# GpSimd's gathers also wait for TensorE's signal of the quad two back

## The reference

```python
x = _layernorm(x + _L0_gnn_ref(...))   # attention: scores from K[src], Q[dst] and edge features; sums of V[src]*score by dst
x = _layernorm(x + _L1_gnn_ref(...))   # mean of x[src] and maximum of relu(x @ W_pool + b)[src] by dst, two matmuls, batch norm
x = _layernorm(x + _L2_gnn_ref(...))   # sum of ci * x[src] by dst, a matmul
x = _layernorm(x + _L3_gnn_ref(...))   # sum of edge_weight * (x @ W)[src] by dst, bias, norm
```

## Time and profile before

| | before |
|---|---|
| median of three runs | 4448.03 us |
| profiled execution | 4444.6 us |
| its span | 4442.8 us |
| GpSimd busy | 3209.6 us (72%) |
| TensorE busy | 2622.2 us (59%) |
| VectorE busy | 1994.1 us (45%) |
| ScalarE busy | 1397.3 us (31%) |
| first gather of pass 1, 2, 3, 4 | 42.1, 1191.9, 2321.7, 3379.0 us |

### The profile page before, as it was taken

How to read it: one execution, slowest core, us unless ns; L and a number is a source line. 1 busy time by engine, 2 the same in 40 slices (tenths; PEclk the granted TensorE clock), 3 DMA queues, 4 the chain that set the end, 5 groups by cost and what they waited for, 6 DMA issues and landing times.

```text
span 4442.8 us, 56823 instructions
## 1 busy us (share of the span) xinstructions
PE 2622.2 (59%) x15402; PEld 2238.4 (50%) x15402; DVE 1994.1 (45%) x4498; ACT 1397.3 (31%) x4325; POOL 3209.6 (72%) x3366
## 2 busy tenths in 40 slices
PE   6777887887676667666756643343344333344435
PEld 5666666666566666666634433333343333333334
DVE  3766666666576666666661111111124222222225
ACT  1222222224444444444453322222222222222223
POOL 4777777776277777777757777777776777777776
PEclk7999889897588888888875555555555555555556
DMA  6876676766333333333312122211122111121112
GB/s 192 221 189 184 182 185 182 185 185 170 96 102 99 99 99 99 101 100 99 97 40 40 40 40 40 40 40 40 40 44 51 40 40 39 40 40 39 40 40 55
DMA packets 337337, 409.95 MB, mean 92 GB/s; under 512 B 212209, under 2 KB 248676, under 8 KB 336942
## 3 DMA queue, kind: packets, MB, share of 16 engines
q0 software_dynamic: 133120, 245.58, 23.3%
q1 hardware_dynamic: 203917, 160.75, 13.5%
HBM read 386.26 MB, written 19.77 MB: 91 GB/s over the span
## 4 chain that ended last, share of the span: by engine, by line
POOL 32%; issue 27%; PE 23%; DVE 11%; DMA 5%; ACT 1%; SPq 1%; ACTq 0%; DVEq 0%; POOLq 0%
POOL rows L547 31%; PE bank L639 18%; DVE same L1534 5%; DVE same L1234 3%; DMA rows<-kv_table,src_idx 2%; PE bank L840 1%; DMA rows<-pair_table,src_idx 1%; DVE prod L1306 1%; DVE score L1308 1%; POOL acc_max L574 1%; DVE prod L1304 1%; PE bank L684 1%; PE bank L652 0%; PE bank L653 0%; PE bank L744 0%
## 5 line engine op out<-in xcount | busy, mean ns | idle before, releaser
L639 PE MATMUL bank<-same,rows 128*96 128x128 f32 x4992 | 1086.0, 389 | 1123.9 <-issue 1044.0
L639 PEld LDWEIGHTS bank<-same,rows 128*96 128x96 f32 x4992 | 926.3, 248 | 1257.4 <-issue 1251.5
L547 POOL DMA_INDIRECT rows<-kv_table,src_idx x832 | 793.7, 954 | 318.8 <-issue 238.9
L547 POOL DMA_INDIRECT rows<-pair_table,src_idx x832 | 787.0, 946 | 317.5 <-issue 249.2
L927 ACT COPY acc<-bank 96x511 f32 (+1 forms) x832 | 481.0, 578 | 1647.1 <-PE bank L639 1645.8
L547 POOL DMA_INDIRECT rows<-h_table,src_idx x832 | 790.2, 950 | 272.3 <-issue 253.3
L547 POOL DMA_INDIRECT rows<-ci_table,src_idx x832 | 785.0, 944 | 261.6 <-issue 253.3
L1234 DVE TENSOR_TENSOR same<-bank,rank_col 128x512 f32<-128x512 f32 x624 | 422.9, 678 | 842.7 <-PE bank L639 842.7
L1534 DVE TENSOR_SCALAR same<-iota_s,rank_col,src_hi 128x128 f32<-128x128 f32 x832 | 240.4, 351 | 754.5 <-PE bank L639 754.3
L639 PEld LDWEIGHTS bank<-same,msg 128*105 128x105 f32 x1664 | 232.1, 197 | 306.6 <-DVE same L1234 199.2
L652 PE MATMUL bank<-weights,first_only 97*128 97x96 f32 x1664 | 355.5, 299 | 38.6 <-DMA first_only<-q_table 32.8
(11 more groups left out here) (169 smaller groups left out, 3241.4 us busy)
## 6 DMA issues: line engine op xcount, KB each, us to landing
first_only<-in_attr_cols SPq DMA_DIRECT2D x104, 384.0 KB
first_only<-q_table SPq DMA_DIRECT2D x832, 48.0 KB
first_only<-rank_rows SPq DMA_DIRECT2D x104, 256.0 KB
first_only<-keep_rows SPq DMA_DIRECT2D x104, 192.0 KB, 3.1
rows<-kv_table,src_idx POOLq DMA_INDIRECT x832
rows<-pair_table,src_idx POOLq DMA_INDIRECT x832
rows<-ci_table,src_idx POOLq DMA_INDIRECT x832
rows<-h_table,src_idx POOLq DMA_INDIRECT x832
```

Source lines behind the costliest of these rows:

```text
L547: pool.indirect_dma_start(rows[:, k, j, 0:width], None, table, bass.IndirectOffsetOnAxis(ap=src_idx[:, t:t + 1], axis=0)).then_inc(rows_in ...
L639: mm = pe.matmul(out[0:nrow, here], left(j), right(j), start=(j == 0), stop=(j == TQ - 1), skip_group_check=True)
```

## The change

`edge_pass_pool` gets two more arguments, a semaphore `paced` and a number `behind`. Before the first gather of quad q it waits, besides the free buffer, until `paced` has been raised for quad q - 2. With `behind = 2` quads 0 and 1 of a pass have no such wait. `paced` is `q_done` in pass 1, `turn_done` in pass 2 and `agg_done` in passes 3 and 4, where it is also the semaphore of the buffer wait.

```diff
-        def edge_pass_pool(pool, table, width, freed):
+        def edge_pass_pool(pool, table, width, freed, paced, behind):
             for q in range(NQ):
                 k = q % GQ
                 wait(pool, freed, q - GQ + 1)
+
+                wait(pool, paced, q - behind + 1)
                 for j in range(TQ):
...
-            edge_pass_pool(pool, kv_table, KV, msg_done)
+            edge_pass_pool(pool, kv_table, KV, msg_done, q_done, 2)
...
-            edge_pass_pool(pool, pair_table, PAIR, passes[1].agg_done)
+            edge_pass_pool(pool, pair_table, PAIR, passes[1].agg_done, turn_done, 2)
...
-            edge_pass_pool(pool, ci_table, F, passes[2].agg_done)
+            edge_pass_pool(pool, ci_table, F, passes[2].agg_done, passes[2].agg_done, 2)
...
-            edge_pass_pool(pool, h_table, F, passes[3].agg_done)
+            edge_pass_pool(pool, h_table, F, passes[3].agg_done, passes[3].agg_done, 2)
```

## The result

| | before | after |
|---|---|---|
| median of four runs each | 4446.34 us | 4475.46 us |
| lowest to highest | 4444.19 to 4450.7 us | 4472.38 to 4478.1 us |
| profiled execution | 4444.6 us | 4478.0 us |
| its span | 4442.8 us | 4476.2 us |

The ratio on record is 1.0061, 95% interval 1.0049 to 1.0072: 29 us slower by the medians, where 12.8 were forecast.

A forecast was written before the change was run, and what follows sets the result against it. GpSimd's gather issue rate was taken as the bound. Delays at the starts of pass 1 (5.6) and pass 2 (7.2), all else 0, sum to +12.8 us: 4461 us predicted, range 4448 to 4473 (forecast alone 4456 to 4467).

The forecast's parts named there:

- Who bounds the kernel: All passes: GpSimd's issue rate, 5.0 us a quad; its lateness in mid-pass reaches the pass end one for one.
- the tail: End of pass 1, quads 201 to 207: held by the new wait, but 7.4 us against 18, cost 0.
- Pass 1, start, +5.6: Pass 1, quads 10 and 11: quad 11 starts 5.57 us late, all reaching consumers; bounds 3.3 to 6.5.
- rival A: Pass 1 and 2 starts: held gathers free the DMA engines, giving part of the delay back; 4452 to 4456, chance 0.18.
- Pass 2, start, +7.2: Pass 2, quad 2: waits for the late first turn, starting at 1209.08 instead of 1201.85; all 7.2 us reach the tail.
- Rival B: Pass 1 mainly: gathers get shorter, so not slower, about 4444 us; chance 0.06.
- Passes 3 and 4, middle, 0: Signal of two quads back comes 1.72 us before the gather, 0.73 is needed: wait already met, cost 0.
- The added wait as an instruction: From each pass's fifth quad, about 816 extra sequencer instructions: taken as 0, bounds 0 to 326 us.
- The comparison of 0.73 with 1.72: Middle of passes 3 and 4: signal-to-gather time 0.73 us is below the signal's 1.72 us lead, so cost 0.
- Rival C: All passes: each of 816 added wait instructions shows at 30 ns, 25 us on top of 12.8, about 4486; chance 0.08.
- Rival D: Middle of passes 3 and 4: a signal needs over 1.72 us; 0.5 us excess costs 103 us, 4564; chance 0.02.
- Rival E: Whole kernel: the new wait never binds, 4448 us; chance 0.02.

The follow-up runs named there:

- the repeat: The changed kernel run again with no edit, beside the kernel before: 4473.81 us against 4442.84, ratio 1.0077.
- the kernel with two more: The changed kernel plus two always-met waits per quad, against the kernel before in 18% slower jobs: ratios 1.0028, 0.9990, 0.9997.

## Why the prediction was wrong

- *Who bounds the kernel.* Right for passes 3 and 4 (7.4 us more from first to last gather in each, of which 6.5 and 7.4 reach the end) and for the 7.2 us of pass 2. In pass 1 the tail changed what arrived (below).
- *Pass 1, start, +5.6.* The number agrees, in part by luck. At quad 20 GpSimd is 5.6 us late in the first profile (6.5 - 0.9), but 3.5 in the repeat and 3.3 with the new wait alone, which is what rival A allowed for. (Quad 10 began at 120.0; 118.9 was forecast.) The pass as a whole cost 6.1, 5.8 and 5.4 us in three profiles, the last with the early quads left alone: there the same loss arose at quads 14 to 16. So it doesn't hang on quads 10 and 11; GpSimd loses its lead over TensorE wherever the wait first applies. And the tail, which the forecast took to be neutral, added to the delay or gave it back: with the new wait alone the whole of it, at a granted clock of 0.61 to 0.83 where the repeat had 0.50.
- *Pass 2, start, +7.2.* Right: 7.25 and 7.1 us, gone when the wait was left out there. The signal to gather time of 0.27 us held.
- *Rival A.* Fell in pass 2: the first turn waited 18.23 us for rows, as before. In pass 1 two of three profiles gave what it said.
- *Rival B.* Fell: gathers of pass 1 weren't shorter (median 949 ns against 946, the longest 2206 against 1767).
- *Passes 3 and 4, middle, 0*, and ***The added wait as an instruction***: **this is the step that failed.** It said "So the sequencer had already handed over a dozen gathers and three waits. I take 0." The dozen gathers were handed over past waits that the gathers carried. In the change the sequencer stands at a separate wait until TensorE signals, and in the middle of passes 3 and 4 the lead shrinks from a dozen gathers to 1.6 us. The comparison of 0.73 with 1.72 asked when the *first* gather is ready, and it was; the second one, once in 104 gathers 3.75 us behind the signal and due at 2.9, was not asked about. Cost: 14.6 us of gaps (3.0 in the middle of pass 2, 5.8 in each of passes 3 and 4). Carried instead, the same wait costs none of it.
- *Rival C, every wait instruction shows, 4486.* Nearest in time, wrong in mechanism: with 816 instructions that were met at once the median is 1.3 us higher, within the noise.
- *Rival D, the wait binds in the middle of passes 3 and 4.* Nearest in mechanism, far off in size (4564): a signal does need more than the lead there, but only for the second gather and only once in 104 gathers.
- *Rival E, the wait never binds.* Fell at both starts.
- *The rule of the Trainium skill* ("Perfetto Trace Analysis", Sequencer Loop and the timeline of a sequencer-only instruction) said that a control instruction holds the sequencer; I weighed it for the first gather only. The waits executed at TensorE's signals bear it out (2610.5 behind 2610.43), and so do the 4.5 us for which the sequencer stands at such a wait in the kernel with two more.
- *The sum.* 33.4 = 0.9 (first gather of all) + 6.1 + 7.25 + 14.6 + 4.6 left over, about the 4.4 us by which the gathers of passes 2 to 4 are longer. The repeat has 2.9 of those, the kernel with both waits from quad 14 none, and they are not explained.

**Open:** what makes the handing over of gather 113 + 104k of a pass long (in the window around it the transfers show gathers only, no load of instructions), what makes gathers longer in some profiles, what sets the clock in the tail of pass 1, and what one wait from quad 14 or the wait for the quad three back does in a usual job.

## What to carry to other kernels

Two waits before one instruction make one of them an instruction of its own, which stops the sequencer's running ahead until it is met; a wait that is met "in time" for the first instruction behind it can still be late for the second. Count what the lead hides, not only when the wait is met: let the later signal be carried by the work instruction (here it alone was enough, since it implies the other), or wait for something that came long ago. And look at the longest gap of a line, not its median, which was the same before and after.

## What the hardware showed

- A wait instruction that is met costs 17 ns on the sequencer and nothing measurable in time (4444.0 against 4442.69 us for 816). One that isn't cuts the lead.
- Handing over has a long case once every 104 indirect gathers: 3.7 us from a separate wait's end to the second gather behind it, in all 18 gaps of the changed kernel's profile and in the long jobs too (4.0 in one gap of the kernel with both waits from quad 14), against 2.9 or less otherwise. It is covered when the wait ended 3.8 us ahead, and with a dozen gathers handed over ahead no gap shows.
- One program took 4443 us in some jobs and 5217 to 5264 us in others. In a long one three engines went on together 2.9 to 3.1 us after the matmuls that they waited for. There, holding GpSimd to two quads ahead of TensorE by a carried wait gives about 2% back. Why is open.
